# Routed experts on gathered rows instead of on all tokens, in a two-layer attention and feed-forward kernel

## What is computed

```
g, u       = x @ sw1.T, x @ sw2.T                 # shared, hidden size 1024
shared_out = silu(g) * u @ sw3.T
scores     = sigmoid(x @ router_w.T)              # (1024 tokens, 8 experts)
_, top_idx = top_k(scores + expert_bias, 2)
top_scores = scores[top_idx] / (sum of the two + 1e-9)
combine    = zeros(T, 8), top_scores added at top_idx
h1, h2     = split(einsum('td,ehd->teh', x, w12)) # hidden size 128 for each expert
out_e      = einsum('teh,edh->ted', silu(h1) * h2, w3)
return shared_out + einsum('ted,te->td', out_e, combine)
```

## Time and profile before

| | us |
|---|---|
| median of 3 runs (1697.99 to 1700.66) | 1698.25 |
| the profiled execution's own time | 1698.53 |
| its span, first to last instruction | 1696.7 |
| PE busy / PE weight loads busy | 1620.9 / 1401.2 |
| DVE busy | 1124.4 |
| ACT busy | 925.8 |
| POOL busy | 573.2 |
| mean granted TensorE clock | 0.997 of full speed (2.4 GHz) |

### The profile page before, as it was taken

The page is one execution under the profiler, slowest core; times in us unless marked ns, Lnnn a source line. Parts: engine busy times, 40 slices in busy tenths (PEclk is TensorE's granted clock), DMA queues, the critical chain, the costliest instruction groups (busy, mean ns, idle before and its releaser), DMA issues.

```text
span 1696.7 us, 30650 instructions
## 1 busy us (share of the span) xinstructions
PE 1620.9 (96%) x11016; PEld 1401.2 (83%) x11016; DVE 1124.4 (66%) x2651; ACT 925.8 (55%) x1937; POOL 573.2 (34%) x514
## 2 busy tenths in 40 slices
PE   8899999999999999899999999999999989999997
PEld 7888889889888677688878898898988877767886
DVE  6767667676636778454776676766756478765557
ACT  5666555565444577533356655556554437773343
POOL 2545444454460102011136355443555320030120
PEclk9999999999999999999999999999999999999999
DMA  3010000000110432111011000000002124220110
GB/s 128 20 50 17 26 1 16 25 17 1 48 58 19 72 52 69 45 38 38 10 50 41 1 17 26 16 25 0 17 1 66 39 42 70 46 73 1 38 47 25
DMA packets 35838, 58.89 MB, mean 35 GB/s; under 512 B 8032, under 2 KB 22768, under 8 KB 34672
## 3 DMA queue, kind: packets, MB, share of 16 engines
q1 hardware_dynamic: 35712, 57.23, 12.9%
HBM read 41.34 MB, written 3.42 MB: 26 GB/s over the span
## 4 chain that ended last, share of the span: by engine, by line
PE 71%; DVE 13%; ACT 8%; issue 5%; POOL 2%; ACTq 0%; DMA 0%; DVEq 0%; POOLq 0%; SPq 0%
PE ps L344 18%; PE ps L346 17%; PE ps L345 16%; PE ps L1000 4%; PE ps L1017 4%; PE ps L960 4%; DVE nmax L1554 2%; ACT E L1212 2%; PE ps L809 2%; POOL E L1892 1%; ACT PT_h L1194 1%; DVE On L1474 1%; PE ps L996 1%; DVE PT_l L1531 1%; PE ps L735 1%
## 5 line engine op out<-in xcount | busy, mean ns | idle before, releaser
L1212 ACT ACTIVATE E<-ps,nmax 128x128 f32<-128x128 f32 (+7 forms) x256 | 188.9, 741 | 209.5 <-DVE nmax L1554 209.1
L1889 POOL TENSOR_SCALAR E<-E,mixc 128x128 f32<-128x128 f32 (+7 forms) x128 | 96.8, 757 | 369.7 <-DVE mixc L1524 369.7
L1554 DVE TENSOR_REDUCE nmax<-ps 128x1 f32<-128x128 f32 (+7 forms) x256 | 183.1, 748 | 12.8 <-PE ps L784 12.6
L1324 ACT ACTIVATE PT<-ps 128x512 f32<-128x512 f32 x288 | 154.8, 601 | 58.9 <-PE ps L1000 56.7
L1892 POOL TENSOR_TENSOR E<-E 128x128 f32<-128x128 f32 (+7 forms) x128 | 182.4, 1425 | 10.7
L1875 POOL TENSOR_TENSOR Fw_l<-Fw_raw,Fw_h 128x768 fp32r<-128x768 f32 x48 | 88.5, 1844 | 253.4 <-ACT Fw_h L1264 252.6
L344 PE MATMUL ps<-V_h,PT_h 128*128 128x256 f32 x576 | 167.0, 290 | 0.0
L345 PE MATMUL ps<-V_l,PT_h 128*128 128x256 f32 x576 | 162.8, 283 | 0.0
L346 PE MATMUL ps<-V_h,PT_l 128*128 128x256 f32 x576 | 162.7, 282 | 0.0
L344 PE MATMUL ps<-K_h,Q_h 128*128 128x512 f32 (+3 forms) x384 | 147.7, 385 | 9.0 <-ACT E L1212 5.3
L344 PE MATMUL ps<-XT_h,Fw_h 128*128 128x512 f32 x384 | 153.0, 398 | 2.8 <-DVE XT_l L1405 2.8
(11 more groups left out here) (210 smaller groups left out, 4625.8 us busy)
## 6 DMA issues: line engine op xcount, KB each, us to landing
Fw_raw<-in_fa SPq DMA_DIRECT2D x48, 256.0 KB, 2.6
Wa_raw<-in_wa SPq DMA_DIRECT2D x8, 1024.0 KB, 5.0
Wo_raw<-in_wo SPq DMA_DIRECT2D x8, 512.0 KB, 3.5
Fw_raw<-in_fb SPq DMA_DIRECT2D x32, 128.0 KB, 2.7
KS<-QK_h SPq DMA_DIRECT2D x56, 64.0 KB
QS<-QK_h SPq DMA_DIRECT2D x56, 64.0 KB
Xn<-in_x SPq DMA_DIRECT2D x4, 512.0 KB, 4.3
Fw_raw<-w2s SPq DMA_DIRECT2D x16, 128.0 KB, 2.7
```

Source lines behind the costliest of these rows:

```text
L1212: nc.scalar.activation(e[:, 0:w], ps[m][:, 0:w], ACT.Exp, bias=nmax[:, s % 4, m:m + 1], accum_out=lsum[:, s % 4, m:m + 1]).then_inc(exp_do ...
L1324: nc.scalar.activation(PT[:, at:at + HALF], bank1(RING1 + n % RING1), ACT.Exp, scale=SCALE1).then_inc(t_used, 1)
L1554: nc.vector.tensor_reduce(nmax[:, s % 4, m:m + 1], ps[m][:, 0:(s % NT + 1) * P], AX.X, ALU.max, negate=True).then_inc(nmax_ready[m], 1)
L1889: nc.gpsimd.tensor_scalar(e2, e2, mixc[:, n % 4:n % 4 + 1], 1.0, ALU.mult, ALU.mult).then_inc(mix_scaled, 1)
```

## The change

The routed experts leave the row of steps, which now ends at 31 (`CHUNKS` 24 to 16). In their place:

1. **Router and places.** It starts one step earlier and has 40 small DVE instructions instead of 20 (parts 0 to 7). `rank_tokens` on PE counts, with 9 small bf16 matmuls, how many earlier tokens chose the same expert. From that DVE computes `place_i`, the row of each of the 2048 (token, choice) pairs in a list sorted by expert in which each expert begins at a multiple of 128, `expert`, the owner of each of 23 tiles of 128 rows (packed, six owners to a number), and `share`, the two weights of each token.
2. **Scatter.** POOL issues 16 indirect DMAs (128 rows of 1032 bytes each) that write the rows of `X`, with a destination number in two added columns, to `xs` in DRAM. `xs` is set to empty rows beforehand by one DRAM to DRAM copy of 3.0 MB on SP. SP then loads `xg` from it: 6 DMAs of 2 to 5 tiles, in three semaphore groups.
3. **23 tiles of one expert each** (`routed`). For a tile PE turns the rows (2), makes gate and up (6 matmuls of 256 columns with the tokens stationary), turns the gated product (1), and makes down (3 matmuls of 256 columns). The expert's weights `E_h`, `E_l` are found by register: four loads of `expert` into registers ahead of the loop, then register arithmetic. The loop is a pipeline of 27 iterations, in each of which PE works on four different tiles. ACT has four instructions a tile and DVE three. The result is copied over `xg`.
4. **Scatter back.** POOL issues 23 indirect DMAs, one a tile, to `ys` in DRAM at row 2 * token + choice. SP loads `yg` with 4 DMAs of 512 KB.
5. **Sums.** `add_experts` adds the two rows of each token to `X`, with `share`: 16 instructions on DVE, then statistics and the layer norm. In batch 0 they stand between the units and in steps 2 to 5 and 7 of batch 1's first group; ACT's two square roots stand in step 6. In batch 1 they stand at the end of the program.
6. **Place of the tiles** (`moe_at`): after step 31 in batch 0; in batch 1 after step 27, so that shared steps 28 to 31 come behind them.
7. **Weights.** All 8 experts' weights are loaded at once after the third layer norm (4 DMAs of 786 KB), split by ACT in steps 16 to 19 (two instructions of 768 columns a step) and by POOL. The low parts of chunks 13 to 15 go from POOL to DVE (`split_low`).
8. **`X` of the next batch** is loaded by a DMA of its own; `add_bias` adds in place and moves behind POOL's work of the first group. Half of `sum_w2` moves from steps 4 to 7 to units 4, 6 and 8 of batch 0's projections.

```diff
-                if s >= S_ROUTED and i % 2 == 0:
-                    prior = max(p for p in TAKEN if p < s and chunk_of(p)[1] == h)
-                    pe.wait_ge(y_taken, TAKES * b + 2 * TAKEN.index(prior) + i // 2 + 1)
...
+    def moe_at(b):
+        return STEPS if b + 1 < B else STEPS - QUAD
...
+            def turn_tokens(k):
...
+                if k == 0:
+                    keep_clock(xt_bank[0], 8)
+                pe.wait_ge(xg_in[load], 16 * (len(XG_LOADS[load]) - 1) * (b + 1))
+                for c in range(KC):
+                    mm = nc.tensor.transpose(xt_bank[k % 2][:, tile(c)], xg[:, k, tile(c)], ident[:])
...
+            pe.wait_ge(er_lo, EXPERTS * b + EXPERTS)
+            pe.wait_ge(rt_dve, R_B * b + R_EXPERT)
+            pe.nop(nofuse=True)
+            packs_e = [pe.value_load(expert[0:1, q:q + 1], min_val=0, max_val=(EXPERTS ** PACK) - 1) for q in range(PACKS)]
...
+            for i in range(TILES + 4):
+                if i < TILES:
+                    turn_tokens(i)
+                if i < 2:
+                    down(b, moe_at(b) - 2 + i)
+                if 0 <= i - 3 < TILES:
+                    turn_gated(i - 3)
+                if 0 <= i - 1 < TILES:
+                    gate_up_tile(i - 1, owner(i - 1))
+                if i >= 4:
+                    down_tile(i - 4, owner(i - 4))
...
+            sp.wait_ge(er_lo, EXPERTS * b + EXPERTS)
+            sp.nop(nofuse=True)
+            sp.wait_ge(sc_out, 16 * TOP * NT * (b + 1))
+            for i, ends in enumerate(XG_LOADS):
+                for k0, k1 in zip(ends, ends[1:]):
+                    sp.dma_start(xg[:, k0:k1], d["xs"].rearrange("(k p) n -> p k n", p=P)[:, k0:k1]).then_inc(xg_in[i], 16)
+            if b + 1 < B:
+                sp.wait_ge(down_mm, STEPS * b + STEPS + H_RING)
+                load_x(b + 1)
+            sp.wait_ge(yr_out, 16 * TILES * (b + 1))
...
+            if part == 0:
+                dve.wait_ge(yg_in[h], 32 * (b + 1))
+                dve.wait_ge(y_taken, 2 * b + h + 1)
...
+                ins = nc.vector.scalar_tensor_tensor(out=X[:, t, 0:HID], in0=yg[:, t, part * HID:(part + 1) * HID],
+                                                     scalar=share[:, part, t:t + 1], in1=X[:, t, 0:HID], op0=ALU.mult, op1=ALU.add)
...
+            for t in range(NT):
+                for c in range(TOP):
+                    nc.gpsimd.indirect_dma_start(d["xs"], bass.IndirectOffsetOnAxis(place_i[:, c, t:t + 1], 0), X[:, t, :],
+                                                 None).then_inc(sc_out, 16)
+            for k in range(TILES):
...
+                pool.wait_ge(ry_copy, TILES * b + k + 1)
+                pool.nop(nofuse=True)
+                nc.gpsimd.indirect_dma_start(d["ys"], bass.IndirectOffsetOnAxis(dest_i[:, k:k + 1], 0), xg[:, k, 0:HID],
+                                             None).then_inc(yr_out, 16)
```

More of the change, by code:

```diff
@@ L303, in program @@
     rt_dve = sem("rt_dve")
+    moe_in = sem("moe_in")
+    xs_init = sem("xs_init")
+    er_in = [sem(f"er_in{i}") for i in range(ER_LOADS)]
+    er_hi = sem("er_hi")
+    er_lo = sem("er_lo")
+    rank_mm = sem("rank_mm")
+    sc_out = sem("sc_out")
+    xg_in = [sem(f"xg_in{i}") for i in range(len(XG_LOADS))]
+    rx_ps = sem("rx_ps")
+    rx_hi = sem("rx_hi")
+    rx_lo = sem("rx_lo")
+    rg_mm = sem("rg_mm")
+    rs_done = sem("rs_done")
+    rm_done = sem("rm_done")
+    rh_ps = sem("rh_ps")
+    rh_hi = sem("rh_hi")
+    rh_lo = sem("rh_lo")
+    rd_mm = sem("rd_mm")
+    ry_copy = sem("ry_copy")
+    tri_done = sem("tri_done")
+    dest_done = sem("dest_done")
+    yr_out = sem("yr_out")
+    yg_in = [sem(f"yg_in{i}") for i in range(2)]
+    xd_in = sem("xd_in")
+    y_first = sem("y_first")
     filled = sem("filled")
@@ L894, in ffn @@
                     wait_xt(b, k, 1)
+                if first and s == moe_at(b):
+                    routed(b)
+                if s == S_SHARED + QUAD + 2:
+                    pe.wait_ge(rt_dve, R_B * b + R_RANK)
                 gate_up(b, s)
@@ L897, in ffn @@
                     transpose_x(b, k, 1)
-                if s >= first + 2:
+                if s == S_SHARED + 2:
+                    router(b)
+                elif s == S_SHARED + 3:
+                    turn_logits(b)
+                if s >= first + 2 and not (first and moe_at(b) <= s < moe_at(b) + 2):
                     if s == S_SHARED + QUAD + 2:
@@ L901, in ffn, with rank_tokens @@
                     down(b, s - 2)
-                if s == S_SHARED + QUAD - 1:
-                    router(b)
-                elif s == S_SHARED + QUAD:
-                    turn_logits(b)
+                if s == S_SHARED + QUAD + 1:
+                    rank_tokens(b, s)
+            if first and moe_at(b) == STEPS:
+                routed(b)
+        def rank_tokens(b, s):
+            pe.wait_ge(tri_done, 2 * b + 2)
+            pe.wait_ge(rt_dve, R_B * b + R_BOTH)
+            pe.wait_ge(gu_used, STEPS * b + s + 2)
+            out = ps[2 + (s + 1) % 2][:, 0:RANKS].rearrange("p (t e) -> p t e", e=EXPERTS)
+            nc.tensor.matmul(out[:, 0:NT], tri[:, 0], both[:], start=True, stop=True, skip_group_check=True)
+            for t in range(NT):
+                mm = nc.tensor.matmul(out[:, t + 1:], tri[:, 1], both[:, t:t + 1].to_broadcast([P, NT - t, EXPERTS]),
+                                      start=False, stop=True, skip_group_check=True)
+            mm.then_inc(rank_mm, 1)
@@ L1223, in attn0_group @@
                     scale_ba(it + 1)
+                if b and not out and s == 6:
+                    for h in range(2):
+                        ln_sqrt(b - 1, 3, h)
                 if b == 0 and not out:
@@ L1283, in ffn @@
                     ffn_split(b, s + 2)
-                if s == last - 2:
+                if s == last - 2 and first == 0:
                     ln_sqrt(b, k, 0)
@@ L1391, in _ @@
             ffn(b, S_SHARED, STEPS, 3)
[L1392 to L1393 removed]
+            for h in range(2):
+                if b + 1 < B:
                     x_parts(b + 1, 0, h)
[L1395 removed]
+                else:
+                    ln_sqrt(b, 3, h)
     @block.vector
@@ L1564, in attn0_group @@
                 project_out(s, 1)
+                if b and not out:
+                    if 2 <= s <= 5:
+                        add_experts(b - 1, *((0, 2), (1, 0), (1, 1), (1, 2))[s - 2])
+                    elif s == 7:
+                        for h in range(2):
+                            layernorm(b - 1, 3, h)
                 if b == 0 and not out:
@@ L1648, in ffn @@
         def ffn(b, first, last, k):
             for s in range(first, last):
-                if s == last - 1:
+                if s == last - 1 and first == 0:
                     layernorm(b, k, 0)
@@ L1865, in _ @@
                     x_parts(b + 1, 0, h)
-            finish(b, 3, STEPS - 1)
-            stats(b, 3, NT - 1)
-            moments(b, 3, 1)
-            layernorm(b, 3, 1)
+            else:
+                for h in range(2):
+                    for part in range(TOP + 1):
+                        add_experts(b, h, part)
+                for h in range(2):
+                    layernorm(b, 3, h)
     @block.gpsimd
```

438 lines of the change are left out of this document (334 added, 104 removed).

## The result

| | before | changed |
|---|---|---|
| median of the runs, us | 1698.12 (1697.67 to 1700.66, 4 runs) | 1675.43 (1674.39 to 1677.00, 4 runs) |
| profiled execution / its span | 1698.53 / 1696.7 | 1674.55 / 1672.7 |
| mean granted clock | 0.997 | 0.992 |

The ratio is 0.9865, with a 95% interval of 0.9853 to 0.9877. The forecast was 1672.7.

What follows compares the result with a forecast made beforehand. PE, busy 96% of the span, was taken as the bound. Terms -135.4 + 91.0 + 2.5 + 2 + 1.5 + 5 + 7.6 = -25.8 from 1698.5 gave 1672.7 us, range 1652 to 1714.

Steps and rivals of the forecast that it cites:

- Steps removed: Routed steps on PE: 16 a batch at 4.23 us go, 67.7 us a batch, 135.4 us saved in two batches.
- a tile 1.6 us: Routed tiles on PE: 1.42 us of matmuls and transposes, taken as 1.6 with register instructions; tile stages +91.0 in all.
- the four register loads: Loads of tile owners into PE's registers ahead of the tiles: 0.6 us each, 2.4 us a batch.
- The wait for the rows: PE ahead of the tiles: scatters 1.4 us each, rows at +56.4; no wait in batch 0, 2.5 us in batch 1.
- Shared steps: Steps beside the router: counting matmuls and longer DVE router chain cost 1 us a batch, +2; expert splits fit ACT's idle time.
- Between the batches: Turn to batch 1: uncovered transposes and split +1.5; expert sums in time with 6 us spare; group 0 +5, bounds 0 to 12.
- "Nothing" for the bias and the sums of `w2`: Bias moved behind POOL's group 0, where POOL idles, and half the w2 sums moved into units: no change in time.
- The end: From the last steps to the span's end: sums, statistics and norms on DVE make 21.9 us of 14.3, +7.6; yg covered.
- Rival 1: POOL's DMAs become the bound at 2.7 us each: longer waits for rows and returns, 1737 us; chance 0.17.
- Rival 2: Tiles longer than their matmuls, by register arithmetic or the tile's turn: 2.2 us an iteration, +30, 1703 us; chance 0.15.
- Step 0 to 16 and the rest of batch 1: Stretches from step 0 to 16 in batch 0 and from group 0 to step 16 in batch 1: 0 predicted.
- The clock: Sign of a wrong forecast: granted clock of 1.2 GHz in a routed stage; no term holds it, since PE never rests.

Runs made afterwards that it cites:

- e0_again: The changed kernel, unaltered, run once more in a later set on another chip: 1669.70 us, ratio 0.9833 to the kernel before.
- e3: Changed kernel with each tile's expert a constant, without register loads or arithmetic (leaves out part of the reference): 1660.41 us, ratio 0.9777 to before.
- e5: Changed kernel with every tile's rows scattered twice, first to a spare array nobody reads: 1735.73 us, ratio 1.0225 to the kernel before.
- e10: Changed kernel with ACT and DVE serving the turned gated product before the turned rows in each tile iteration: 1674.90 us, ratio 0.9858 to before.
- e4: Changed kernel with 8 scatters to xs instead of 16, leaving out every token's second choice: 1662.36 us, ratio 0.9791 to the kernel before.
- e8: Changed kernel with batch 0's last layer norm moved from step 7 of batch 1's first group to steps 8 and 9: 1664.48 us, ratio 0.9805 to before.
- e1: Changed kernel with POOL adding the output bias ahead of its first mixing in batch 0, as before the change: 1671.90 us, ratio 0.9844 to before.
- e2: Changed kernel with the six sums of w2 back in steps 4 to 7 of batch 0's group 0: 1670.32 us, ratio 0.9826 to before.

## Why the prediction was right

The forecast was 2.7 us under the result and the sum holds, -25.8 against -24.0 in the span. The main mechanism was right: PE's work is what the time follows. That it came so close is in part luck: two errors of some 6 us cancel, the 5.6 us that batch 0 gained ahead of its first feed-forward step and the pauses. e0_again, which had no pauses, is 3.0 us under the forecast.

- **Steps removed, a tile 1.6 us**: right in kind. The tiles took 1.73 and 1.67 us with PE 92 and 95% busy; the matmuls alone gave 1.42 by the earlier trace rows. The excess over that has two parts: 0.11 to 0.15 is the registers (e3), the rest stands without them as well. Batch 0's stage gained 23.5 instead of 20.7 us: the removed steps were 68.92 us a batch and not 67.7 (780.54 to 849.46 in the earlier trace rows), which the prediction took too small by 1.2, and the four register loads, put at 2.4, show nothing there. In batch 1 1.23 us of "issue" stand ahead of the keepers, but only in runs with pauses (e5 and e10 too); e0_again has none there, so the loads alone cost nothing that a trace shows.

```profile
1591.22 0.49 PE L779 MATMUL ps<-ident_r 128*128 128x512 f32 x1 [1.23 <-issue]
```

- **The wait for the rows**: the figure of 2.5 us was met by e0_again with 2.65 us, and in the result pauses had used it up. The rows came when forecast: 56.1 us after step 16 against 56.4. PE was ready at 53.4 against 53.9, but by two errors that cancel: step 27 came 1.7 us later than before, and the register loads took nothing instead of 2.4. The scatters were taken as 1.4 us each, between the bounds of 0.33 and 2.7 from the earlier trace rows; they are 1.27 apart in most cases and 1.34 in the mean. The wait's real price is higher than its length, by the stretch at the lower clock behind it, which no term has. The rule of the Trainium skill ("DMA: Bandwidth & Descriptors", anatomy of one DMA on the SWDGE path) would have made a wait of 17 us if its 2.3 us were the distance of two; by these rows it is not that distance, and the page gives it as the latency of one.
- **Shared steps**: +2 was charged, +3.4 came by e0_again, and +13.3 in the result, of which 10 are the pauses and what followed them. In batch 1 5.5 came back in the next row of the table: 2.8 since the rows had landed meanwhile, 1.4 by the clock that then stayed up, the rest since PE stood less far behind than the late product shows. This step failed: the prediction looked at what the router adds on DVE and has no term for stops of PE, ACT and DVE in the steps that the scatters run beside. That the scatters make them is not shown; without pauses they cost these steps nothing (e4). PE's wait for the counts is small:

```profile
734.74 0.50 PE L408 MATMUL ps<-XT_h,Fw_h 128*128 128x512 f32 x1 [0.96 <-DVE rank L2090]
```

- **Between the batches**: the experts' sums were in time in batch 0. Group 0 was charged 5 and cost 7.8, inside the bounds of 0 and 12; e8 names nearly half of it. "DVE is the idler engine" was the wrong reading: in that group DVE is the start of a chain over POOL to PE.
- **"Nothing" for the bias and the sums of `w2`**: wrong by 5.6 us to the good. POOL's idle time was looked at, and not what its long instruction did to DVE: 2.5 us at the first mixing factor by e1. The rest lies in group 0 (71.88 us before, 68.66 now), where the sums moved and where the trace of before has a stretch at the lower clock at 68.3 and this one hasn't; e2 doesn't tell the two apart.
- **The end**: +7.6 predicted, +8.3 measured. `yg` had been issued 16 us before its sums.
- **Rival 1** (POOL's DMAs decide) was off by its price. At twice the number e5 comes to 1735.73, by chance near the 1737 that it gave: POOL's own time would make 40 us of it, the rest goes with the stops, which the rival hadn't. **Rival 2** (registers) is true in its cause and about a fifth of its size.
- **Step 0 to 16 and the rest of batch 1**: nothing was forecast; -0.7 and +3.2 came. Single stretches of 3.4 us at the lower clock lie there (at 553.0 in the trace of before, at 1373.5 in this one), which may be the first and part of the second; e8, without the one at 1373.5, still is 1.8 us over the kernel before in that part. What makes these 1.8 stays open.
- **The clock**: no term held a fall behind a pause or a wait, though the text named one in a routed stage as a sign of an error. The result has none there, e0_again has one, behind the wait for the rows.

Open: what makes the pauses of the scatters' last third, and why they come on some occasions alone. They cost 5.7 us (1675.43 - 1669.70, of two occasions), and no run removed them on an occasion that had them. A small fetch on the instruction queue stands at the same place in both kinds of trace (at 757.5 in the result, at 757.2 in e8), so it doesn't tell them apart.
